# A four-stage conditioned residual stack: the up projection in three rounded passes, its bias folded away, the norm's squares on ScalarE

## The reference

```
x0 = x  (128 samples of 128 tokens x 512);   each sample has a subject (of 8), a category (of 64), a language (of 9) and a delta_t
x1 = x0 + x0 @ W0[subject].T + b0[subject]
x2 = x1 + rotate(x1)          pairs of tokens, by an angle and amplitude that depend on delta_t
x3 = x2 + x2 @ W2[category] + b2[category]
h  = relu(x3 @ W1[language] + b1[language])            512 -> 128
y  = x3 + h @ Wup[language] + bup[language]            128 -> 512
out = x3 + (y - mean(y)) * rsqrt(var(y) + 1e-5) * gamma[language] + beta[language]
```

## Time and profile before

| | us |
|---|---|
| median of 3 runs | 1187.41 (1184.76 to 1187.66) |
| the profiled execution, its own time | 1190.44 |
| its span, first to last instruction | 1188.6 |
| busy in the span: DVE, ACT, POOL | 1014.9, 584.5, 831.0 |
| mean granted TensorE clock | 0.981 of full |
| read from HBM, written | 256.06 MB, 33.55 MB |

### The profile page before, as it was taken

How to read it: one execution, slowest core, us unless ns; L and a number is a source line. 1 busy time by engine, 2 the same in 40 slices (tenths; PEclk the granted TensorE clock), 3 DMA queues, 4 the chain that set the end, 5 groups by cost and what they waited for, 6 DMA issues and landing times.

```text
span 1188.6 us, 27887 instructions
## 1 busy us (share of the span) xinstructions
PE 1125.9 (95%) x5904; PEld 913.0 (77%) x5904; DVE 1014.9 (85%) x1464; ACT 584.5 (49%) x925; POOL 831.0 (70%) x792
## 2 busy tenths in 40 slices
PE   3899999999999999999998999989998999899996
PEld 2678878887888777788786888868886888788884
DVE  5588888888889888889988888888888888888887
ACT  3355555555454545454554445455545545545542
POOL 6286666676778787678767666866766778766774
PEclk8999999999999999999999899999999999999998
DMA  7977776877777778767768776787788777867782
GB/s 245 422 256 261 252 245 216 257 237 256 249 238 252 221 247 277 256 214 248 249 214 270 248 237 216 246 278 239 218 258 271 215 253 244 273 215 250 238 254 87
DMA packets 96407, 291.83 MB, mean 246 GB/s; under 512 B 11328, under 2 KB 11712, under 8 KB 78272
## 3 DMA queue, kind: packets, MB, share of 16 engines
q1 hardware_dynamic: 95472, 289.52, 74.6%
q10 hardware_dynamic: 720, 0.14, 0.1%
HBM read 256.06 MB, written 33.55 MB: 244 GB/s over the span
## 4 chain that ended last, share of the span: by engine, by line
SPq 39%; PE 34%; issue 17%; DMA 4%; DVE 3%; POOL 1%; DVEq 1%; ACT 0%; ACTq 0%; POOLq 0%
SPq L196 6%; SPq L202 6%; SPq L208 5%; DMA b_in<-b 4%; PE ps_l L814 4%; PE ps_l L765 4%; PE ps_l L804 4%; PE ps_hT L834 4%; PE ps_l L782 4%; PE ps_y L843 3%; PE ps_l L808 3%; PE ps_mix L793 3%; SPq L199 3%; SPq L211 3%; SPq L205 3%
## 5 line engine op out<-in xcount | busy, mean ns | idle before, releaser
L650 DVE TENSOR_TENSOR w_lo<-w_in,w_hi 128x1024 fp32r<-128x1024 f32 x256 | 317.9, 1282 | 0.0
L388 POOL TENSOR_TENSOR x_lo<-x_in,x_hi 128x512 fp32r<-128x512 f32 x128 | 165.8, 1295 | 194.0 <-DVE w_lo L650 189.1
L497 ACT ACTIVATE w_hi<-w_in 128x1024 fp32r<-128x1024 f32 x256 | 255.4, 1045 | 8.4 <-PE ps_l L808 8.3
L382 POOL TENSOR_TENSOR w_in<-w_in,ident 128x512 f32<-128x512 f32 x128 | 164.3, 1284 | 76.9 <-DMA w_in<-W 76.1
L462 ACT ACTIVATE ps_diag<-ident,cos 128x128 f32<-128x128 f32 x128 | 47.6, 372 | 298.0 <-DVE mix L627 297.6
L793 PEld LDWEIGHTS ps_mix<-mix,x 128*128 128x128 f32 x1024 | 133.9, 192 | 73.1 <-issue 68.9
L405 POOL TENSOR_TENSOR x3b<-x,bup_sb 128x512 f32<-128x512 f32 x128 | 163.1, 1274 | 11.3 <-DVE x L672 11.3
L412 POOL TENSOR_TENSOR x<-x,beta_sb 128x512 f32<-128x512 f32 x128 | 170.7, 1334 | 0.0
L765 PE MATMUL ps_l<-w_hi,x_hi 128*128 128x512 f32 x512 | 153.5, 423 | 3.1 <-issue 3.1
L834 PE MATMUL ps_hT<-x3T,w_in 128*128 128x128 f32 x1024 | 139.4, 280 | 13.8 <-ACT x3T L518 13.8
L678 DVE TENSOR_TENSOR ps_y<-ps_y,x3b 128x512 f32<-128x512 f32 x128 | 89.5, 699 | 73.4 <-PE ps_y L843 72.4
(11 more groups left out here) (86 smaller groups left out, 1696.3 us busy)
## 6 DMA issues: line engine op xcount, KB each, us to landing
w_in<-W SPq DMA_DIRECT2D x128, 1024.0 KB, 6.1
b_in<-b SPq DMA_DIRECT2D x136, 256.0 KB, 5.9
x_in<-xT SPq DMA_DIRECT2D x128, 256.0 KB, 4.8
w_in<-W SPq DMA_DIRECT2D x128, 256.0 KB, 2.7
out<-yb SPq DMA_DIRECT2D x128, 256.0 KB, 5.4
w_in<-W0T SPq DMA_DIRECT2D x8, 1024.0 KB, 5.0
bup_sb<-bup SPq DMA_DIRECT2D x1, 2560.0 KB, 11.7
wup_sb<-Wup SPq DMA_DIRECT2D x1, 2560.0 KB, 15.5
```

What stands on the lines that cost most here:

```text
L388: pool.tensor_tensor(x_lo[s % 2][:, :], x_in[s % XB][:, :], x_hi[s % 2][:, :].bitcast(fp32), ALU.subtract).then_inc(x_lo_made, 1)
L497: act.activation(w2_hi[:, halves[n]], w2_in[s % WB][:, halves[n]], ACT.Copy).then_inc(w2_hi_made, 1)
L650: dve.tensor_tensor(w2_lo[:, half], w2_in[s % WB][:, half], w2_hi[:, half].bitcast(fp32), ALU.subtract).then_inc(w2_lo_made, 1)
```

## The change

The up projection gets the same treatment as the large ones: ScalarE rounds h to h_hi, GpSimd makes h_lo, Wup is split once at the start into wup_hi and wup_lo (five parts each), and three fp32r products are summed. The up bias is no longer added to x3 on GpSimd. Instead b2[category] + bup[language] is computed for every sample at the start (one-hot matmuls on TensorE), stored to a scratch tensor in HBM, and loaded in the place of b2, so x3 already holds bup. What must not see bup is corrected: the copy of x3T subtracts it (four biased instructions, one for each 128 columns; down waits for each of them), and bup is taken off the beta table, which goes through HBM once. The mean comes from an accumulator of the add, the variance from a Square instruction with an accumulator on ScalarE. The bup table is not loaded; Wup is loaded earlier, gamma and beta after SP's step 0.

```diff
+        wup_hi = sb("wup_hi", [A, L * D], fp32r)
...
-        bup_sb = sb("bup_sb", [P, L * D])
+        wup_lo = wup_sb[:, :].bitcast(fp32r)
+        minus_bup = sb("minus_bup", [P, C * L])
...
-        onehot = hT[:, :]
+        onehot = h[:, :]
...
+        bias_rows = nc.dram_tensor("bias_rows", [B, D], fp32, kind="Internal").ap()
+        beta_rows = nc.dram_tensor("beta_rows", [L, D], fp32, kind="Internal").ap()
+        id_rows = yb[0][:, 0:2 * B].bitcast(i32)
+        category_onehot, language_onehot = (yb[0][:, n * B:(n + 1) * B] for n in (2, 3))
+        b2_rows, bup_rows, beta_in = yb[1], yb[2], x3[X3B - 1]
+        bias_sum = b2_in[1]
...
+        wup_parts = [slice(n * WD // 2, min((n + 1) * WD // 2, L * D)) for n in range(-(-L * D // (WD // 2)))]
...
-                cat = category_of(sp, s) if k > 0 else sp.value_load(icols[0:1, 2:3], min_val=0, max_val=K - 1)
+                sample = sample_of(sp, s) if k > 0 else 0
...
-                sp.dma_start(b2_in[j % BB][:, :], b2[bass.ds(cat, 1)].rearrange("o d -> (o d)").partition_broadcast(P))\
+                sp.dma_start(b2_in[j % BB][:, :],
+                             bias_rows[bass.ds(sample, 1)].rearrange("o d -> (o d)").partition_broadcast(P))\
...
+            sp.dma_start(id_rows[:, 0:B], category.partition_broadcast(P)).then_inc(rows_loaded, 16)
+            sp.dma_start(id_rows[:, B:2 * B], language.partition_broadcast(P)).then_inc(rows_loaded, 16)
+            sp.dma_start(b2_rows[0:K, :], b2).then_inc(rows_loaded, 16)
+            sp.dma_start(bup_rows[0:L, :], bup).then_inc(rows_loaded, 16)
+            sp.dma_start(beta_in[0:L, :], beta).then_inc(rows_loaded, 16)
...
-            load_b2(0, 0, 0)
...
+            sp.dma_start(wup_sb[:, :], Wup.rearrange("p l d -> p (l d)")).then_inc(wup_loaded, 16)
...
-            sp.dma_start(bup_sb[:, :], table(bup)).then_inc(bup_loaded, 16)
...
+            sp.wait_ge(bias_stored, 16)
+            load_b2(0, 0, 0)
...
-            sp.dma_start(wup_sb[:, :], Wup.rearrange("p l d -> p (l d)")).then_inc(wup_loaded, 16)
...
-            sp.dma_start(gamma_sb[:, :], table(gamma)).then_inc(gamma_loaded, 16)
-            sp.dma_start(beta_sb[:, :], table(beta)).then_inc(beta_loaded, 16)
...
+            sp.wait_ge(beta_made, 1)
+            sp.dma_start(beta_rows, beta_in[0:L, :]).then_inc(beta_stored, 16)
...
-            for s in range(AHEAD):
+            step(0, 0, 0)
+            sp.dma_start(gamma_sb[:, :], table(gamma)).then_inc(gamma_loaded, 16)
+            sp.wait_ge(beta_stored, 16)
+            sp.dma_start(beta_sb[:, :], table(beta_rows)).then_inc(beta_loaded, 16)
+            for s in range(1, AHEAD):
...
-                pool.wait_ge(mean_made, s + 1)
-                pool.tensor_tensor(var_eps[:, :], mean_var[:, 1:2], eps[:, :], ALU.add).then_inc(var_eps_made, 1)
+                pool.wait_ge(squares_made, s + 1)
+                pool.tensor_scalar(var_eps[:, :], square_sum[:, :], 1.0 / D, LN_EPS, ALU.mult, ALU.add)\
+                    .then_inc(var_eps_made, 1)
...
-            def add_up_bias(s, lang):
...
-                pool.wait_ge(x3_made, s + 1)
-                if s >= 2:
-                    pool.wait_ge(y_made, s - 1)
-                pool.tensor_tensor(x3b[s % 2][:, :], x3[s % X3B][:, :], bup_sb[:, bass.ds(lang * D, D)], ALU.add)\
-                    .then_inc(x3bias_made, 1)
+            def rest_of_h(s):
...
+                if s >= 1:
+                    pool.wait_ge(up_done, s)
+                pool.wait_ge(h_hi_made, s + 1)
+                pool.tensor_tensor(h_lo[:, :], h[:, :], h_hi[:, :].bitcast(fp32), ALU.subtract).then_inc(h_lo_made, 1)
...
-                pool.wait_ge(x3bias_made, s + 1)
+                pool.wait_ge(y_made, s + 1)
...
+            pool.wait_ge(rows_loaded, 16 * 5)
+            pool.tensor_tensor(beta_in[0:L, :], beta_in[0:L, :], bup_rows[0:L, :], ALU.subtract).then_inc(beta_made, 1)
...
-            pool.wait_ge(bup_loaded, 16)
...
-            lang = None
...
+                if s >= 1:
+                    rest_of_h(s - 1)
+                if s < LAST - 1:
...
-                lang_before, lang = lang, language_of(pool, s)
-                add_up_bias(s, lang)
...
-                    add_beta(s - 1, lang_before)
+                    add_beta(s - 1, language_of(pool, s - 1))
...
-            add_beta(LAST, lang)
+            rest_of_h(LAST)
...
+            add_beta(LAST, language_of(pool, LAST))
...
-            def relu_hT(s, lang):
+            def relu_h(s, lang):
...
+                if s >= 1:
+                    act.wait_ge(h_lo_made, s)
+                act.wait_ge(hT_done, s + 1)
+                act.activation(h[:, :], ps_hT[:, :], ACT.Relu, bias=b1_sb[:, bass.ds(lang, 1)]).then_inc(h_made, 1)
...
+            def round_h(s):
...
-                act.wait_ge(hT_done, s + 1)
-                act.activation(hT[:, :], ps_hT[:, :], ACT.Relu, bias=b1_sb[:, bass.ds(lang, 1)]).then_inc(hT_made, 1)
...
-            def copy_x3T(s):
+                act.wait_ge(h_made, s + 1)
+                act.activation(h_hi[:, :], h[:, :], ACT.Copy).then_inc(h_hi_made, 1)
...
+            def square(s):
...
+                act.wait_ge(y_made, s + 1)
+                if s >= 1:
+                    act.wait_ge(scaled_made, s)
+                act.activation(neg_mean[:, :], y_sum[:, :], ACT.Copy, scale=-1.0 / D).then_inc(mean_made, 1)
+                if s >= 1:
+                    act.wait_ge(var_eps_made, s)
+                act.wait_ge(mean_made, s + 1)
+                act.activation(squares[:, :], ps_y[s % 2][:, :], ACT.Square, bias=neg_mean[:, 0:1],
+                               accum_out=square_sum[:, :]).then_inc(squares_made, 1)
...
+            def round_wup(n):
...
+                act.activation(wup_hi[:, wup_parts[n]], wup_sb[:, wup_parts[n]], ACT.Copy).then_inc(wup_hi_made, 1)
...
+            def copy_x3T(s, lang):
...
-                act.activation(x3T[:, :], ps_x3T[:, :], ACT.Copy).then_inc(x3T_made, 1)
+                for c in range(C):
+                    act.activation(x3T[:, c * N:(c + 1) * N], ps_x3T[:, c * N:(c + 1) * N], ACT.Identity,
+                                   bias=minus_bup[:, bass.ds(lang + c * L, 1)]).then_inc(x3T_made, 1)
...
+            act.wait_ge(bup_turned, 1)
+            act.activation(minus_bup[:, :], ps_y[0][:, 0:C * L], ACT.Copy, scale=-1.0).then_inc(minus_bup_made, 1)
+            act.wait_ge(bias_summed, 1)
+            act.activation(bias_sum[:, :], ps_y[1][:, :], ACT.Copy).then_inc(bias_copied, 1)
+            act.wait_ge(bias_copied, 1)
+            act.dma_start(bias_rows, bias_sum[:, :]).then_inc(bias_stored, 16)
...
+            act.wait_ge(wup_loaded, 16)
+            for n in range(2):
+                round_wup(n)
...
+            act.wait_ge(minus_bup_made, 1)
+            act.wait_ge(ids_made, 2)
+            lang = None
...
-                if s >= 1:
-                    relu_hT(s - 1, language_of(act, s - 1))
+                lang_before, lang = lang, language_of(act, s)
+                if s >= 1:
+                    relu_h(s - 1, lang_before)
+                if s >= 2:
+                    square(s - 2)
+                if s >= 1:
+                    round_h(s - 1)
...
+                if s == 0:
+                    for n in range(2, len(wup_parts)):
+                        round_wup(n)
...
-                copy_x3T(s)
+                copy_x3T(s, lang)
...
-            relu_hT(LAST, language_of(act, LAST))
+            relu_h(LAST, lang)
+            round_h(LAST)
+            square(LAST - 1)
+            square(LAST)
...
+                    dve.wait_ge(rows_loaded, 16 * 5)
+                    link(dve.tensor_copy(category_onehot, id_rows[:, 0:B]))
+                    link(dve.tensor_copy(language_onehot, id_rows[:, B:2 * B]))
+                    dve.tensor_scalar(category_onehot, category_onehot, cols[:, 0:1], None, ALU.is_equal)\
+                        .then_inc(rows_made, 1)
+                    dve.tensor_scalar(language_onehot, language_onehot, cols[:, 0:1], None, ALU.is_equal)\
+                        .then_inc(rows_made, 1)
...
-            def statistics(s):
+            def rest_of_wup(n):
...
+                dve.wait_ge(wup_hi_made, n + 1)
+                dve.tensor_tensor(wup_lo[:, wup_parts[n]], wup_sb[:, wup_parts[n]],
+                                  wup_hi[:, wup_parts[n]].bitcast(fp32), ALU.subtract).then_inc(wup_lo_made, 1)
...
+            def add_x3(s):
...
-                dve.wait_ge(x3bias_made, s + 1)
...
-                dve.tensor_tensor(y[:, :], y[:, :], x3b[s % 2][:, :], ALU.add).then_inc(y_made, 1)
-                dve.wait_ge(y_made, s + 1)
-                dve.bn_stats(stats[:, :], y[:, :]).then_inc(stats_made, 1)
-                dve.wait_ge(stats_made, s + 1)
-                dve.bn_aggr(mean_var[:, :], stats[:, :]).then_inc(mean_made, 1)
+                if s >= 1:
+                    dve.wait_ge(mean_made, s)
```

(50 more changed lines are left out.)

30 lines of the change are left out of this document (22 added, 8 removed).

## The result

The changed kernel takes 1197.19 us (median of 6, 1194.42 to 1199.18) against 1187.54 for the kernel before: ratio 1.0071, 95% interval 1.005 to 1.0092. The forecast was 1183 with 1174 to 1195; it is slower, and above the range. The profiled execution has a span of 1195.5 us, 6.9 more than before. The medians are 9.65 apart: the profiled execution of the kernel before lay 2.9 us above its median and that of the changed kernel 0.1, so what follows places 6.9 us and not the rest.

What follows compares the result with a forecast made beforehand. SP's issue list, nearly equal to TensorE's pace, was taken as the bound. Start -1.3, steps to the first subject change -0.9, 661 to 726 us -0.5, last fourteen steps -2.2, end +0.7: -4.2, giving 1183 us, range 1174 to 1195.

Steps and rivals of the forecast that it cites:

- What bounds the kernel: SP's list of DMAs and register loads, 8.8 us a sample with loop turns, nearly equal to TensorE's 8.55.
- the distance of the W2 loads: Sign on SP's queue: from load 17 to load 72 of W2 in 493 us, within 2.
- The zero of the 168 to 660 stretch: SP's loop keeps the same number of value loads and DMAs, so this stretch stays as long: 0.
- The start: Up to the early rotations: later tables and added small work shift the start by -1.3 us, bounds -4 and +10.
- Covered by the table that is awaited anyway: At the start: added work moves rotations 1 and 2 by about 2 us, hidden by the wait for the table.
- The rival for this: At the start: GpSimd stands at a late beta table, deciding after about 60.5; +10.5 at the rotation, 1195 us, chance 0.10.
- "Cost 0" for ScalarE: On ScalarE: 1.9 to 2.6 us added per sample, including four biased copies, stays hidden at no cost.
- The 0.18 of the up projection: On TensorE: three fp32r matmuls replace two fp32 pieces, saving 0.18 us per sample; step 8.55 becomes 8.37.
- Late steps: More steps above 8.4 than now, at the end of each stretch of twelve loads, with the fold late at +0.5.
- GpSimd's new tolerance: On GpSimd: the W2 fold may start at rotation +0.5 instead of -0.75, 1.2 us more lead for TensorE, once per stretch.
- third table load: On ScalarE: Square or Identity evicts Sin's function set, two loads of 1.28 us per step; about 1235 us, chance 0.04.
- collision of GpSimd with the splits: Variance, power, h_lo or beta meet VectorE's splits every step, delaying w_lo by 0.2 or more beyond its room; 1200, chance 0.04.

Runs made afterwards that it cites:

- three separate edits of SP's list: Kernel before with two register loads moved into the subject-change branch, 1170.72 us; SP's loop over 60 samples instead of 12, 1174.73; output store behind load of x, 1168.56.
- the four edits of the changed kernel that leave the list in SP's loop alone: Changed kernel with tables before step 0, 1192.99 us; TensorE's register load before the rotation, 1189.70; x3T in one copy, 1193.45; tables around sample 2's loads, 1190.30.
- three other traces of the kernel before: Kernel before with shorter SP list, 1170.72 us; two turns of SP's loop, 1174.73; output store behind load of x, 1168.56.
- The edits that undo these two causes: Changed kernel with table transfers moved up to sample 2's x and W2 loads, 1190.30 us; with TensorE's register load ahead of the rotation, 1189.70.
- all three edits: Changed kernel with early tables, two SP register loads moved into the subject-change branch, and TensorE's register load ahead of the rotation: 1148.28 us, ratio 0.9676.

## Why the prediction was wrong

**What bounds the kernel** was right, and it is the part most strongly shown: three separate edits of SP's list make the kernel before 1.2 to 1.6% faster, and the distance of the W2 loads, forecast as 493 us within 2, was 493.15. The zero of the 168 to 660 stretch goes with it. That it came within 0.01 is luck: in the four edits of the changed kernel that leave the list in SP's loop alone it was 491.3 to 495.8.

**The start failed**, as the term "I take -1.3": it came out at +7.0, inside its bounds of -4 and +10. I let the tables be asked for at 45; they were at 48. I let beta land 13 us and 1.5 later, at 59.5; its copy took 15.4, from 48.3 to 63.7. From the landing to rotation 3 I counted 3.55 us, it took 5.0: between the landing and the start of the add alone lie 1.2, a register load and register operations that the sum left out. "Covered by the table that is awaited anyway" took the wait for something given: the reorder is what made the table the last to come, by leaving the DMA engines little used from 40 to 45 us. The rival for this had the mechanism and the point of decision (beta after 60.5) and got 0.10; the start went by it, with +5.0 of its +10.5 us at rotation 3. The +2.0 behind it are the half clock, which was in no term, and since three other traces of the kernel before have it too, it is not shown that the change costs them: in part they are luck of the profiled pair.

**"Cost 0" for ScalarE failed.** I asked whether the data of the four copies comes in time for the down projection, and it does: the matmuls of L948 stall on it only in the steps at changes of subject, for 10.9 us in all (13.8 before). I did not ask what is queued behind those waits on TensorE. It is a register load, 0.3 us that were hidden at +0.16 and are just hidden at +0.85; and it meets the store's slow window. Between rotations 4 and 13 this made +2.4 us where the forecast had -0.5; over the run it is the 10.8 us, part of them where SP would have held TensorE anyway.

**The 0.18 of the up projection** was 0.12. The tie was named ("nothing more would be gained") and has the size at fault: x1 ends at 8.26 after the rotation instead of 8.22, and the rotation follows it by 0.17, not 0.15.

**Late steps** came as forecast, with GpSimd's new tolerance: 416 us in the changed kernel, fold late as at 407 us in the earlier trace rows:
```profile
416.89 1.28 POOL L416 TENSOR_TENSOR w_in<-w_in,ident 128x512 f32<-128x512 f32 x1 [2.68 <-DMA w_in<-W]
...
418.13 1.30 POOL L446 TENSOR_TENSOR x<-x,beta_sb 128x512 f32<-128x512 f32 x1
...
418.20 3.45 DVE L741 TENSOR_TENSOR w_lo<-w_in,w_hi 128x1024 fp32r<-128x1024 f32 x2
```
Both splits take 3.45 us beside one add, where they took 4.03 beside two; the step is 9.08 us for 9.99, though the fold starts 1.20 us behind the rotation, for 0.83. By the Trainium skill (SBUF — State Buffer, SBUF: two separate sides) the instruction that starts second waits for the first one's whole length; the add starts 0.07 us before the splits and takes 1.30, which gives an estimate of 1.2 for VectorE. The trace has 3.45 - 2.35 = 1.1, close to it. At the changes of subject the fourteen steps rose from 36.4 us over 8.55 each to 43.2 over 8.43. I read this as W0 on SP's clock, to which TensorE only comes sooner; it is not shown, and the clock is a second reading: between 80 and 1130 us the stretches with a granted clock of 0.50 add up to 38 us in the changed kernel and to 20 before. The end was +1.0 for +0.7; the last output instruction, which answers to the earlier trace rows:
```profile
1192.12 0.75 DVE L795 SCALAR_TENSOR_TENSOR yb<-ps_y,rstd,x 128x512 f32<-128x512 f32 x1 [0.60 <-POOL rstd L433]
```
No third table load was made, and no collision of GpSimd with the splits showed in ordinary steps; those rivals fell.

Between the forecast change of the span (-4.2) and the measured one (+6.9) lie 11.1 us; start and first stretch make 12.1 of them, the other terms gave 1.0 back. The edits that undo these two causes are worth 6.9 us (tables) and 7.5 (register load) by the medians, together more than the loss of 9.65. Part of what they free the kernel before had lost too: with all three edits R3 is 61.2, where it was 63.7. How much that is in all is not separated.

## What to carry to other kernels

Where a wait moves or is split, list what its engine's queue holds behind it, register loads and branches too: they cost nothing only as long as the queue runs ahead of the engine. Where a profile's chain is on the issuing queue, shorten or reorder that list before touching arithmetic: two register loads moved into a branch were worth 17 us here, and the change showed its worth only after that: 1155 us with this edit and TensorE's register load moved, 1148 with the tables early as well, against 1171 for the kernel before with the same edit. Several list edits together were not run on the kernel before. When a large load is put off, look at what the DMA engines do in the time that becomes free; and a small transfer that something waits for goes ahead of the large one.

## What the hardware showed

A register load from SBUF takes 0.27 to 0.31 us in the median on every queue, and up to 1.2 us, mostly when it begins 0.75 to 2.0 us behind the issue of the output's 256 KB store from SBUF (means of 0.47 to 0.78 us there in the changed kernel, by quarters of a microsecond). On SP, whose own store it was, the median of the load behind it is 608 ns in the kernel before and 270 with the store moved. With the store behind the load of x those 1.5 us behind the store are at 0.29 again. It strikes several queues at one moment: at 191.25 us of the changed kernel loads of SP, ScalarE and GpSimd that had taken 0.73, 0.88 and 0.89 us end within 0.02 of each other, and one of TensorE's that ended 0.3 earlier had taken 0.91.

From 57 to 67 us of the changed kernel TensorE had matmuls for 1.81 us, and its granted clock was 0.50 in the 5 us from 68 on, 1.2 GHz instead of 2.4. In the kernel before TensorE had matmuls for 2.88 us of the seven from 55 to 62, and with the store behind x for 2.39; the granted clock from 62 to 67 us was 0.95 in the one and 0.50 in the other.
